# A decoder layer on one core: h transposed through one PSUM bank, the waits of TensorE asked in another order, and new instruction orders

## What is computed

```python
x = x + attn(layernorm(x), W_qkv, W_out)              # 16 heads of 16, causal softmax
x = x + xattn(layernorm(x), ctx, mask)                # one head of 256, keys = values = ctx, /16, masked
x = x + ffn(layernorm(x), gate_w, down_w, g_gate, g_down)

def bit_linear(x, w, g):
    xn = rms_norm(x, g)
    xq = activation_quant(xn)      # rows scaled to +-127 and rounded
    wq = weight_quant(w)           # scaled by mean |w|, rounded to -1, 0, 1
    return xq @ wq.T
def ffn(x, ...):                   # 256 -> 2 * 704 -> 256
    gate, up = split(bit_linear(x, gate_w, g_gate))
    return bit_linear(gate * sigmoid(gate) * up, down_w, g_down)
```

## Time and profile before

| | |
|---|---|
| three runs | 208.86, 209.68, 209.47 us; median 209.47 |
| the profiled execution, its time | 208.5 us |
| its span, first to last instruction | 206.5 us |
| granted TensorE clock, mean | 0.999 |
| TensorE busy | 186.9 us, 91% |
| VectorE busy | 165.7 us, 80% |
| ScalarE busy | 152.2 us, 74% |
| GpSimd busy | 113.8 us, 55% |
| transfers | 12.82 MB |

### The profile page before, as it was taken

How to read it: one execution, slowest core, us unless ns; L and a number is a source line. 1 busy time by engine, 2 the same in 40 slices (tenths; PEclk the granted TensorE clock), 3 DMA queues, 4 the chain that set the end, 5 groups by cost and what they waited for, 6 DMA issues and landing times.

```text
span 206.5 us, 10407 instructions
## 1 busy us (share of the span) xinstructions
PE 186.9 (91%) x3967; PEld 149.6 (72%) x3967; DVE 165.7 (80%) x522; ACT 152.2 (74%) x438; POOL 113.8 (55%) x258
## 2 busy tenths in 40 slices
PE   3999999999998999999999999999999998885673
PEld 3878688977786778888787879788878776552341
DVE  1335599998895968988998889797979899999982
ACT  2378985858887686879878797977797877575651
POOL 6410328445746362665465575537483558787880
PEclk9999999999999999999999999999999999999999
DMA  5999100101002100020203000202001020300002
GB/s 169 383 342 354 58 3 3 54 3 52 3 0 86 51 3 25 0 78 2 76 0 103 28 29 2 76 2 73 3 26 52 20 63 27 103 5 2 25 25 76
DMA packets 11474, 12.82 MB, mean 62 GB/s; under 512 B 1010, under 2 KB 10674, under 8 KB 11444
## 3 DMA queue, kind: packets, MB, share of 16 engines
q1 hardware_dynamic: 11444, 12.46, 18.6%
HBM read 10.36 MB, written 2.10 MB: 60 GB/s over the span
## 4 chain that ended last, share of the span: by engine, by line
PE 73%; issue 8%; DVE 7%; ACT 7%; POOL 2%; DMA 1%; ACTq 1%; DVEq 0%; SPq 0%; POOLq 0%
PE ps L366 13%; PE ps L350 8%; PE ps L344 8%; PE ps L376 7%; PE ps L451 5%; PE ps L429 5%; PE ps L533 5%; PE ps L466 5%; PE ps L491 5%; PE ps L398 4%; PE ps L479 3%; PE ps L420 2%; PE ps L388 2%; PE ps L550 2%; DVE wg L1411 1%
## 5 line engine op out<-in xcount | busy, mean ns | idle before, releaser
L2006 POOL TENSOR_TENSOR zh<-hh,gd 128x352 f32<-128x352 f32 x32 | 29.9, 949 | 9.9 <-DVE hh L1350 9.6
L366 PE MATMUL ps<-yaT,wqk 128*128 128x128 f32 x256 | 31.9, 278 | 0.6 <-ACT yaT L701 0.5
L1925 POOL TENSOR_SCALAR ve<-mv 128x1 f32<-128x1 f32 x32 | 7.8, 243 | 42.9 <-issue 34.4
L366 PEld LDWEIGHTS ps<-yaT,wqk 128*128 128x128 f32 x256 | 30.2, 194 | 1.6 <-ACT yaT L701 1.2
L1222 DVE TENSOR_REDUCE mx<-ps 128x16 f32<-128x1024 f32 x16 | 19.6, 1224 | 10.2 <-PE ps L398 9.9
L350 PE MATMUL ps<-wg,zT 128*128 128x352 bf16 x128 | 22.7, 312 | 2.9 <-ACT hT L704 1.3
L805 ACT ACTIVATE th_sb<-ps,th 128x352 f32<-128x352 f32 x32 | 17.5, 552 | 6.5 <-PE ps L350 3.1
L1927 POOL TENSOR_TENSOR rs<-ve,neghalf 128x1 f32<-128x1 f32 x32 | 20.5, 641 | 2.7
L762 ACT ACTIVATE pT<-ps 128x512 f32<-128x512 f32 x32 | 17.8, 597 | 4.4 <-PE ps L436 4.3
L701 ACT ACTIVATE v<-ps 64x128 f32<-64x128 f32 x64 | 17.6, 274 | 2.8 <-PE ps L376 2.2
L350 PEld LDWEIGHTS ps<-wg,zT 128*128 128x128 bf16 x128 | 11.3, 97 | 9.9 <-issue 2.3
(11 more groups left out here) (117 smaller groups left out, 486.6 us busy)
## 6 DMA issues: line engine op xcount, KB each, us to landing
ct_in<-ctx_t SPq DMA_DIRECT2D x16, 128.0 KB, 2.2
cn_in<-ctx_n SPq DMA_DIRECT2D x16, 128.0 KB, 2.2
out<-o_out SPq DMA_DIRECT2D x16, 128.0 KB, 1.7
wg<-gate_t SPq DMA_DIRECT2D x1, 1408.0 KB, 8.2
x_in<-x SPq DMA_DIRECT2D x1, 1024.0 KB, 11.5
wd<-down_t SPq DMA_DIRECT2D x1, 640.0 KB, 8.9
wqk<-wqkv_t SPq DMA_DIRECT2D x1, 512.0 KB, 4.0
x_in<-x SPq DMA_DIRECT2D x1, 512.0 KB, 9.0
```

The lines of the kernel that those rows point to most:

```text
L366: last = pe.matmul(qk_ps[:, e * P:(e + 1) * P], wqk[:, c, e * P:(e + 1) * P], yaT[:, t % 2, c, :], start=(c == 0), stop=(c == DC - 1))
L2006: G.tensor_tensor(zh[:, t % 2, part], hh[:, t % 2, part], gd[:, part], ALU.mult).then_inc(ev[f"zh_d{j}"], 1)
```

## The change

Five things. (1) h is transposed in one step, all six chunks into bank 0, and copied out by one ScalarE instruction of 768 columns (`transpose_h`, `keep_hT`); bank 5 is no longer used for it. (2) In TensorE's steps the waits for freed banks and loaded weights are now asked first and the wait for the step's own input last. (3) The first tile is normalised on VectorE (`normalise_first`), which takes the mean off itself, so that GpSimd's `nm` and `sh` of the first tile fall away. (4) The seven identity products become three products of 512 columns on zeros, which wait for a clearing by VectorE and not for the constants; `keep_busy` has 2, 2, 3, 7, 2 and 2 products where it had 4, 4 and 7. (5) All orders are written anew, on every engine, with other waits for banks to suit. SyncE's stores of tiles 1 and 5 move ahead of the context loads of tiles 5 and 9.

```diff
--- before.py
+++ after.py
...
-WARM = 7
+WARM = 3
...
-        hT_ps = [bank(0, 2 * P).bitcast(F16), bank(5, (IC - 4) * P // 2).bitcast(F16)]
+        hT_ps = bank(0, IC * P // 2).bitcast(F16)
...
             def transpose_ya(t, *users):
-                pe.wait_ge(ev["ya_d"], at(t + 1))
                 freed(users)
+                if isinstance(t, int) and t == 0:
+                    pe.wait_ge(ya_first, 1)
+                else:
+                    pe.wait_ge(ev["ya_d"], at(t))
                 transposes(xT_ps, ya[:, t % 2, :], DC, ev["yaT_ps"])
 
             def project_qk(t, *users):
-                pe.wait_ge(ev["yaT_d"], at(t + 1))
-                freed(users)
                 if first(t):
                     pe.wait_ge(wqk_in, 16)
+                freed(users)
+                pe.wait_ge(ev["yaT_d"], at(t + 1))
...
-            def transpose_h_0(t, *users):
-                pe.wait_ge(ev["hq_d"], at(t + 1))
-                freed(users)
+            def transpose_h(t, *users):
                 if first(t):
                     pe.wait_ge(pads_set, 3)
-                transposes(hT_ps[0], hq_halves[:, t % 2, 0:4 * P, 0], 4, ev["hT_ps0"], ident_16)
-
-            def transpose_h_1(t, *users):
+                freed(users)
                 pe.wait_ge(ev["hq_d"], at(t + 1))
-                freed(users)
-                if first(t):
-                    pe.wait_ge(pads_set, 3)
-                transposes(hT_ps[1], hq_halves[:, t % 2, 4 * P:IC * P, 0], IC - 4, ev["hT_ps1"], ident_16)
+                transposes(hT_ps, hq_halves[:, t % 2, :, 0], IC, ev["hT_ps"], ident_16)
...
+            still = hq[:, 0, 0:P]
+            pe.wait_ge(still_set, 1)
+            for _ in range(WARM):
+                pe.matmul(ps[:, 7, :].rearrange("p (n k) -> p n k", k=P), still, still.unsqueeze(1).broadcast_to([P, 4, P]), start=True, stop=True)
             pe.wait_ge(cst_in, 16)
-            for _ in range(WARM):
-                pe.matmul(ps[:, 7, 0:P], ident, ident, start=True, stop=True)
             transpose_ya(0)
             project_qk(0)
+            project_v(0)
             transpose_ya(1)
-            project_v(0)
             scores_q(0)
...
             def step(s):
                 transpose_z(s - 4)
-                scores_q(s, ("exp_d0", s), ("exp_d1", s))
+                scores_q(s, ("exp_d1", s), ("exp_d0", s))
                 readout(s - 1, ("out_d", s - 5))
+                transpose_ya(s + 1, ("zT_d", s - 3))
                 cross_readout(s - 3)
-                transpose_ya(s + 1, ("zT_d", s - 3))
-                gate_up_1(s - 4, ("mx_d", s + 1))
-                gate_up_0(s - 4)
+                gate_up_0(s - 4, ("mx_d", s + 1))
+                gate_up_1(s - 4)
                 transpose_yx(s - 2, ("yaT_d", s + 2))
                 transpose_readout(s - 1, ("x2_d", s - 2))
                 project_qk(s + 1)
-                cross_scores(s - 2, ("v_d", s + 1))
-                transpose_h_1(s - 5, ("h1_d1", s - 3))
-                transpose_h_0(s - 5)
+                cross_scores(s - 2)
                 transpose_max(s, ("h1_d0", s - 3))
                 project_out(s - 1)
-                scores_k(s, ("hT_d1", s - 4), ("hh_d0", s - 3), ("hh_d1", s - 3), ("mT_d", s + 1))
-                down(s - 5, ("k0_d", s + 2), ("k1_d", s + 2))
+                transpose_h(s - 5)
+                scores_k(s, ("mT_d", s + 1), ("hh_d1", s - 3), ("hh_d0", s - 3))
+                down(s - 5)
                 transpose_cross_weights(s - 2, ("x1_d", s))
                 project_v(s + 1)
...
-            keep_busy(2, 4, ("rsum_d", 16), ("oN_d", 16))
...
+            keep_busy(2, 2, ("rsum_d", 16), ("oN_d", 16))
...
-            keep_busy(7, 4, ("tanh_d0", 14), ("h1_d0", 14))
+            keep_busy(5, 2, ("tanh_d1", 14), ("h1_d1", 14))
...
+            def keep_hT(t):
+                act.wait_ge(ev["hT_ps"], t + 1)
                 after(act, ev["d_ps"], t - 1)
+                integers(hT[:, t % 2, :, :].rearrange("p c t -> p (c t)"), hT_ps).then_inc(ev["hT_d"], 1)
...
             act.wait_ge(cst_in, 16)
-            normalise_x(0)
             keep_yaT(0)
+            keep_k_0(0)
             normalise_x(1)
...
+            def normalise_first():
+                dve.wait_ge(rstd1[0], 1)
+                V.tensor_scalar(ya[:, 0, :], x_in[:, 0, :], mv1[:, 0, 0:1], rs1[:, 0:1], ALU.subtract, ALU.mult).then_inc(ya_first, 1)
...
+            V.memset(hq[:, 0, 0:P], 0.0).then_inc(still_set, 1)
...
-                G.tensor_scalar(nm1[:, part], mv1[:, part, 0], -1.0, None, ALU.mult).then_inc(nm1_d[k], 1)
+                if k > 0:
+                    G.tensor_scalar(nm1[:, part], mv1[:, part, 0], -1.0, None, ALU.mult).then_inc(nm1_d[k], 1)
...
+                if k == 0:
+                    return
```

992 lines of the change are left out of this document (482 added, 510 removed).

## The result

The changed kernel takes **214.76 us** (median of four runs, 213.51 to 216.51) where the kernel before takes 209.17 (four runs beside it): ratio 1.027, interval 1.019 to 1.036. Forecast were 207.1 us with a range up to 209.8, so the sign is wrong. The profiled execution is the one of 213.51 us, 5.1 us longer in its span than before's. Executions of one kernel spread more than usual in this case: medians and ranges are of all of them, and the ratios leave out those over 1.5% above the fastest of their kernel.

What follows compares the result with a forecast made beforehand. TensorE was taken to set the loop's pace with VectorE close behind, and VectorE and GpSimd the tail's. Terms -0.1 - 0.6 - 1.3 - 0.4 = -2.4 us, applied to the 209.47 median, gave 207.1 us; 8-in-10 range 204.8 to 209.8.

Steps and rivals of the forecast that it cites:

- the 0.96 us of "issue" at 64.09: First loop steps: 0.96 us wait in mid-product, for nothing on the chip, taken as a reason the change doesn't touch.
- the rivals: Forecast, zeros lifting clock or not, 0.50; all terms near good ends 0.19; VectorE paces instead 0.20; late single copy 0.11.
- D: Slower: single copy of h late before down, 11 steps wait about 0.5 us each; +2.7, 212.2 us; chance 0.11.
- start: Up to third query/key product at 18.58: earlier clock rise mostly lost in the chain; -0.1 us, bounds -0.8 and +0.3.
- ramp: 18 to 56 us: two VectorE operations move behind the first rounded feed-forward input; -0.6 us, bounds -1.5 and +0.5.
- loop: Ten loop steps: excess waits -1.7, exposed copy +1.0, other waits -0.6; -1.3 us, bounds -2.4 and +1.0.
- tail: Kernel's end: earlier GpSimd work -0.6, against an added GpSimd operation and lost copy overlap; -0.4 us, bounds -1.5 and +0.8.
- the good end that the forecast allowed: Start: clock level rises early enough to cut the zeros short; up to 0.8 us gained.
- The exposed copy: Loop: down waits for the 0.82 us copy of h, 0.05 us in eight steps, 0.5 in the tenth, 0.1 in the fifth.

Runs made afterwards that it cites:

- 16 and 48: Changed kernel with 16 more waits under its zero products and 48 instructions of tiny products before the third and fourth transpose_readout waits; 207.22 us, ratio 0.989; repeated 207.69.
- with 16: Changed kernel with 16 already-met semaphore waits added under its three products on zeros; 208.24 us, ratio 0.995.
- four places in all: Kernel before: as it was; 20 instructions fewer, 215.93 us; 70 waits more, 216.07 us; 48 instructions of tiny products in the loop, 209.49 us.
- at 7: Changed kernel with 7 instructions added between its products on zeros; 213.86 us (209.10 to 219.32).

## Why the prediction was wrong

**The step that failed** is the one sentence that the 0.96 us of "issue" at 64.09 is "a reason the change doesn't touch". It is the one row of before that held the outcome. A wait that no engine and no transfer explains, in the middle of a product, has a cause all the same, and this one depends on how many instructions stand ahead of it. The change took 17 out of TensorE's program (the warm products alone 16) and gave each step another order, so every block end landed in another place. The runs showed in its place waits for late instruction blocks: 1.46 and 2.50 us in after, with 1.15 us of lower clock behind the second. None of the rivals has this mechanism, so the chances of all were too high; D, the slower one, had the direction by luck and the wrong cause.

By terms, against the version whose place is good (16 and 48) and the one with 16:

| term | forecast | with 16 | with 16 and 48 | after |
|---|---|---|---|---|
| start, to 18.58 | -0.1 | +0.24 | -0.43 | +2.10 |
| ramp, to 55.95 | -0.6 | -0.06 | +0.20 | +0.23 |
| loop, to the tenth `down` | -1.3 | -0.82 | -2.34 | +1.55 |
| tail | -0.4 | +0.2 | -0.4 | +1.2 |
| sum | -2.4 | -0.4 | -3.0 | +5.1 |

**Start.** The mechanism was right: the zeros begin at 1.04 (forecast 1.1), six records fill 5.49 us (5.1), the first transposes stand at 6.32 as before, the first query/key product takes 2.02 us in place of 2.38, and the first maxima's reduction begins at 12.11, 0.26 later (at most 0.1 was forecast). In the run with 16 and 48 the zeros took 4.38 us and the first transposes began at 5.71: there the level rose sooner, the good end that the forecast allowed. The Trainium skill's turning point that varies from run to run (TensorE: Matmul & The Clock Gate, What's actually happening) is seen here: the six records take 5.49 us in the run with 16 and 4.38 in the one with 16 and 48, whose programs are the same up to there. Failed: the chain to 18.58, by the wait in `scores_q(1)`.

**Ramp.** Mis-sized: -0.6 was forecast for two VectorE operations of 0.67 us that move behind the first rounded input, -0.1 to +0.2 was measured. Where that gain went was not tested.

**Loop.** -0.13 us a step in the steady part (0.09 to 0.15 over all profiled executions). The forecast's -1.3 over ten steps is that size, but its split was wrong. The exposed copy was charged 1.0 us and costs next to nothing: two copies in place of one change a step by 0.03 us, while the mask products stand fixed behind the projection,

```profile
99.12 1.08 PE L469 MATMUL ps<-wo,oT 128*128 128x256 f32 x4
...
100.04 0.50 PE L344 MATMUL ps<-c,hq 128*128 128x128 f16 x6
...
100.47 0.32 PE L423 MATMUL ps<-c 32*64 32x128 bf16 x16
...
100.60 0.82 ACT L697 ACTIVATE hT<-ps 128x768 bf16<-128x768 f16 x1
```

1.35 us with the six transposes inside (1.34 in the disturbed step of the earlier trace rows; 1.01 in the good one, without transposes). The copy is over at 101.42 and `down` starts at 101.56. The 0.82 us forecast for the copy is 0.811. The first two steps are what differs between the kernels: 86.05 less 62.50 is 23.55 us before, 25.61 in after, 23.16 with 16, 21.84 with 16 and 48.

**Tail.** -0.4 in the version with 16 and 48, +0.2 in the one with 16, +1.2 in after: the 0.58 us wait above, and 1.0 us of waiting for the context load more than in the well placed version (1.20 against 0.24), which is the transfer's 3.40 us in the chain where the other's took 2.44. The forecast looked at SyncE's queue in the loop, not in the tail.

**What stays open.** What decides when the next block is asked for. The first comes at 15.3 to 15.9 us or at 17.8 in the kernels with a start like after's, with nothing between; in all runs later ones come between about the end of the block before and some 5 us behind it, and not alike in two executions of one program. Loads that fill the DMA engines at that time (97.6% in the stretch above) may hold it up; but the 2.5 us wait ahead of `down` came with them idle.

## What to carry to other kernels

Look for "issue" waits in the middle of a run of like instructions: count the engine's instructions up to each, and where the remainders by 256 agree, they are likely ends of instruction blocks (here a packet of the instruction queue 2.3 to 2.9 us ahead of each confirmed it), and every edit that changes the number or order of instructions ahead of them can move the time by some per cent either way. Before judging such an edit, time it with a few shifts by harmless instructions, and read its own worth from steps that are run a second time, where these waits didn't appear. Here a measured loss of 2.7% became a gain of 1.1 to 1.4% over a kernel before that was tried at four places in all, and the steady steps were 0.9 to 1.4% shorter at every place.

## What the runs showed of the hardware

- A block of 256 TensorE instructions that was asked for late stopped the engine for 0.4 to 2.5 us; from the packet to the next product it took 2.3 to 2.9 us. The loop's body, some 1110 instructions, ran three more turns in after without a packet (76.1 to 145 us).
- Of eight such stops of 1.9 to 2.5 us, six were followed by the lower clock for 3 us or more (granted clock 0.51 to 0.66 in the stretches behind them; in after at 1.15 us of time); the two of 2.01 and 2.33 us in `scores_q(1)` were not, nor was one of 1.64 us or less.
- The length of the first wait doesn't wear off with the shift: 1.46 and 2.01 us at none, 2.33 at 7, none in five profiled executions with 16.
- The constants landed at 3.07 to 3.18 us in three executions of the kernel before and at 4.15 in one.
- At the start a semaphore wait that has been met and each instruction of a small fp32 product take TensorE 0.11 us; in the score products further on 64 instructions take 0.51 us, 0.008 each.
